# Shared stage rearranged, nine homes for expert weights, square roots in mid-step

## What is computed

```python
# cross-attention: 16 heads of 32, 1601 context rows per sequence
q = qdq(layernorm(x)) @ qdq(wq).T + bq
k, v = split(ctx @ wkv.T + bkv)
x = x + tanh(g_xattn) * (qdq(softmax(q k^T / sqrt(32)) v) @ qdq(wp).T + bp)
# mixture of experts on h = layernorm(x): 32 experts, 4 of them per token
scores = sigmoid(h @ gate_w.T)
top 2 of 4 groups by (scores + gate_bias), then the top 4 experts; weights = scores / sum * 2
slot = running count of tokens per expert, in token order (capacity 128 here)
routed = sum_k weight_k * w2_e(silu(w1_e h) * w3_e h)
shared = (silu(h @ shared_gate) * (h @ shared_up)) @ shared_down
out = x + tanh(g_ffn) * (routed + shared)
```

## Time and profile before

| | us |
|---|---|
| median of 3 runs (lowest, highest) | 3175.16 (3173.58, 3179.16) |
| the profiled execution | 3174.64 |
| its span, first to last instruction | 3172.8 |
| PE busy | 2810.6 (89%) |
| DVE, ACT, POOL busy | 1789.1, 1386.5, 1806.3 |

### The profile page before, as it was taken

One profiled execution on the slowest core, in us unless ns is written; L12 is line 12 of the kernel. 1 busy time (PEld: TensorE's weight loads), 2 busy tenths in 40 slices (PEclk: granted clock), 3 DMA queues, 4 the chain that ended last, 5 costly groups with the idle time before them and its releaser, 6 DMA issues. The chain is left out here.

```text
span 3172.8 us, 43442 instructions
## 1 busy us (share of the span) xinstructions
PE 2810.6 (89%) x14876; PEld 1211.9 (38%) x14876; DVE 1789.1 (56%) x3878; ACT 1386.5 (44%) x2460; POOL 1806.3 (57%) x1570
## 2 busy tenths in 40 slices
PE   5898999899989988998999899989998699996986
PEld 3233333333333333333333333333332354443765
DVE  6576566756665766567567755665653334342221
ACT  3155455644564565455545644564456211010111
POOL 0285567556656676667566656656679032424555
PEclk9798999999999999999999999999999799998999
DMA  3112012210211031112112101211020321222997
GB/s 128 37 45 53 21 35 71 53 31 25 76 53 46 11 101 38 35 40 76 29 34 71 53 21 35 74 53 37 20 65 14 118 71 51 80 80 80 280 290 186
DMA packets 146586, 215.59 MB, mean 68 GB/s; under 512 B 24984, under 2 KB 78232, under 8 KB 146368
## 3 DMA queue, kind: packets, MB, share of 16 engines
q1 hardware_dynamic: 130496, 195.95, 20.5%
q0 software_dynamic: 15872, 16.87, 2.8%
HBM read 126.49 MB, written 34.24 MB: 51 GB/s over the span
## 5 line engine op out<-in xcount | busy, mean ns | idle before, releaser
L1502 POOL TENSOR_TENSOR prob_acc<-prob_acc,probs 128x512 f32<-128x512 f32 x1152 | 1429.3, 1275 | 431.2 <-ACT probs L1031 430.8
L1031 ACT ACTIVATE probs<-s_ps 128x512 f32<-128x512 f32 (+1 forms) x1664 | 937.0, 596 | 758.4 <-PE s_ps L803 727.2
L1245 DVE TENSOR_REDUCE piece_max<-r_all 128x1 f32<-128x400 f32 (+1 forms) x2048 | 1029.2, 566 | 144.9 <-PE r_all L725 138.5
L803 PE MATMUL s_ps<-q_stack,k_flat 97*128 97x512 f16 (+1 forms) x1664 | 633.8, 397 | 66.6 <-ACT probs L1031 58.4
L725 PE MATMUL r_all<-k_flat,q_stack 96*128 96x400 f16 (+1 forms) x2048 | 605.5, 353 | 97.4 <-DVE piece_max L1245 41.2
L817 PE MATMUL o_ps<-probs,v_sb 128*32 128x512 f32 (+1 forms) x3328 | 465.1, 632 | 21.5 <-ACT probs L1031 21.5
L803 PEld LDWEIGHTS s_ps<-q_stack,k_flat 97*128 97x128 f16 (+1 forms) x1664 | 161.3, 101 | 634.8 <-ACT probs L1031 435.7
L1499 POOL COPY prob_acc<-probs 128x512 f32<-128x512 f32 x128 | 72.8, 612 | 490.5 <-PE sum_ps L837 355.9
L725 PEld LDWEIGHTS r_all<-k_flat,q_stack 96*128 96x128 f16 x2048 | 204.4, 101 | 372.5 <-DVE piece_max L1245 122.7
L1534 POOL DMA_INDIRECT slot_rows<-payload,slot x128 | 125.6, 981 | 313.4 <-DVE slot L1432 189.4
L1239 DVE SCALAR_TENSOR_TENSOR k_lo<-r_all,bk_col,k_hi 128x400 f16<-128x400 f32 (+1 forms) x128 | 81.8, 639 | 280.9 <-ACT k_hi L989 280.9
(11 more groups left out here) (193 smaller groups left out, 2719.6 us busy)
## 6 DMA issues: line engine op xcount, KB each, us to landing
k_flat<-k_hi SPq DMA_DIRECT2D x256, 100.1 KB, 2.2
ctx_raw<-in_ctx SPq DMA_DIRECT2D x96, 256.0 KB, 2.8
v_sb<-in_L_ffn_w SPq DMA_DIRECT2D x48, 512.0 KB, 6.3
xin<-in_x SPq DMA_DIRECT2D x16, 1024.0 KB, 5.6
k_flat<-k_lo SPq DMA_DIRECT2D x128, 100.1 KB, 2.2
ctx_hi<-in_L_ffn_w SPq DMA_DIRECT2D x24, 512.0 KB, 6.5
ctx_lo<-in_L_ffn_w SPq DMA_DIRECT2D x24, 512.0 KB, 6.5
q_stack<-q_hi SPq DMA_DIRECT2D x256, 32.0 KB, 1.8
```

The lines of the kernel that those rows point to most:

```text
L803: nc.tensor.matmul(s_ps[j % SBANKS][0:w, :], k_stack[:, g % 2, j, kt * P:kt * P + w], q_stack[:, g % 2, j, :], start=True, stop=True).then ...
L1031: nc.scalar.activation(probs[0:w, slot, j, :], s_ps[j % SBANKS][0:w, :], ACT.Exp).then_inc(probs_ready, 1)
L1245: V.reduce_max(piece_max[:, j * TT + qt, i:i + 1], ps[:, 0:PIECE[i]], X_AXIS).then_inc(free_of(*key), 1)
L1502: last = G.tensor_tensor(prob_acc[:, j, :], prob_acc[:, j, :], probs[:, slot, j, :], ALU.add)
```

## The change

- `ffn_tiles` moves `cum` and `total` behind the second gate and up pair, and puts one `down` tile between the turned h of the next sequence and its logits; the other three `down` tiles come behind the logits.
- On DVE the four routing parts of sequence f + 1 stand between the `add_shared` of sequence f; those of f = 0 come ahead of its first `swiglu`. The slots (`slots_of_experts`) come behind the second `swiglu`.
- `ffn_in` is split. h and x1 of sequences 0 and 1 are loaded ahead of `rows_out(B - 1)`, h of 0 already during the last attention group, into the freed `ctx_lo`; `shared_gate` starts in the last group too.
- Expert weights get 9 homes rather than 4, out of buffers that are free by then; 7 experts are loaded during the shared stage. The slots are read back ahead of the last output. The gathers of the first experts wait for the last `swiglu`, not for the outputs.
- `deviations` goes from the end of its step to behind the second exponential of that step. For the last sequence it goes behind `("logits", 1)`.

```diff
 def ffn_tiles(f):
-    order = gate_tiles(f)
+    gates = gate_tiles(f)
+    order = gates[0:4] + [("cum", f), ("total", f)] + gates[4:]
     if f == 0:
         order += [("oiT", B - 1, c) for c in range(DC)] + [("y", B - 1, t) for t in range(TT)]
-    order += [("cum", f), ("total", f)]
-    order += [("hT", f + 1, c) for c in range(DC)] if f + 1 < B else []
-    order += [("down", f, t) for t in range(TT)]
-    return order + ([("logits", f + 1)] if f + 1 < B else [])
+    down = [("down", f, t) for t in range(TT)]
+    if f + 1 < B:
+        order += [("hT", f + 1, c) for c in range(DC)] + down[0:1] + [("logits", f + 1)]
+        down = down[1:]
+    return order + down
...
-        h_in = (prob_acc[:, :, :], probs[:, 2])
+        h_in = (ctx_lo_flat[:, 0:2 * TT * D].bitcast(FP32).rearrange("p (t d) -> p t d", t=TT), probs[:, 2])
...
+HOMES, EARLY_HOMES, FREE_HOMES = 9, 7, 5
...
             sp.wait_ge(x_quantised, B * TT)
             sp.dma_start(xin[:, :, :], x_v[B - 1]).then_inc(x_again, DMA)
+            key = ("k", B - 1, GROUPS - 1, PIECES - 1)
+            sp.wait_ge(bank_full[ring.last_bank(*key)], ring.done(*key))
+            h_in_of(0)
+            sp.wait_ge(probs_ready, step_of(B - 1, GROUPS - 1, 0) * GH)
+            shared_weights_in(sg, shared_gate)
             sp.wait_ge(acc_summed, B * GROUPS)
-            ffn_in(0)
-            for wt, src in ((sg, shared_gate), (su, shared_up), (sd, shared_down)):
-                sp.dma_start(wt[:, :, :], src.rearrange("(c p) n -> p c n", p=P)).then_inc(shared_in, DMA)
+            shared_weights_in(su, shared_up)
+            h_in_of(1)
+            shared_weights_in(sd, shared_down)
+            for f in range(2):
+                x1_in_of(f)
             rows_out(B - 1)
...
             for f in range(B):
-                if f + 1 < B:
-                    ffn_in(f + 1)
-                if f == B - 2:
-                    expert_weights_in(0)
-                    expert_weights_in(1)
+                if 2 <= f + 1 < B:
+                    h_in_of(f + 1)
+                    x1_in_of(f + 1)
+                if f == 1:
+                    sp.wait_ge(h_out, B * DMA)
+                    sp.wait_ge(x1_out, B * DMA)
+                if 1 <= f <= EARLY_HOMES:
+                    expert_weights_in(f - 1)
+                if f == B - 1:
+                    sp.wait_ge(slots_written, B * TT * TOPK * DMA)
+                    sp.dma_start(e_slots[:, :, :], slot_v).then_inc(e_slots_in, DMA)
                 sp.wait_ge(out_ready, f + 1)
                 sp.dma_start(out_v[f], x1_in[f % 2]).then_inc(out_written, DMA)
             sp.wait_ge(out_written, B * DMA)
             sp.wait_ge(route_ready, B)
-            expert_weights_in(2)
-            expert_weights_in(3)
-            sp.wait_ge(slots_written, B * TT * TOPK * DMA)
-            sp.dma_start(e_slots[:, :, :], slot_v).then_inc(e_slots_in, DMA)
-            for e in range(UN, E):
-                key = ("ey", e - UN)
+            for e in range(EARLY_HOMES, HOMES):
+                expert_weights_in(e)
+            for e in range(HOMES, E):
+                key = ("ey", e - HOMES)
                 sp.wait_ge(bank_full[ring.last_bank(*key)], ring.done(*key))
                 expert_weights_in(e)
...
                 for j in range(GH):
                     exp_of(s, j)
+                    if j == 1 and g == 2 and b + 1 < B and kt == X_STD:
+                        deviations(x_var_ready, b + 2, x_std_ready)
+                    if j == 1 and g == 1 and b and kt == H_STD:
+                        deviations(h_var_ready, b, h_std_ready)
...
-            for f in range(B):
-                for c, part in enumerate((scores_in_groups, best_groups_and_experts, expert_masks, expert_weights)):
-                    swiglu(c)
-                    part()
+            routing = (scores_in_groups, best_groups_and_experts, expert_masks, expert_weights)
+            for part in routing:
+                part(0)
+            for f in range(B):
+                for c in range(FSC):
+                    swiglu(f, c)
+                    if c == FSC // 2 - 1:
+                        slots_of_experts(f)
                 if f == 0:
                     for t in range(TT):
                         tile(("y", B - 1, t))
                     for at in (H_STATS, H_RSTD):
                         h_part(B - 1, at)
+                dve.wait_ge(x1_back[f % 2], (f // 2 + 1) * DMA)
+                for t in range(TT):
+                    if f + 1 < B:
+                        routing[t](f + 1)
+                    add_shared(f, t)
...
             pool.wait_ge(h_out, B * DMA)
-            pool.wait_ge(out_written, B * DMA)
             pool.wait_ge(e_slots_in, DMA)
+            pool.wait_ge(act_ready, B * FSC)
```

More of the change, by code:

```diff
@@ L431, in build @@
         x1_out = sem("x1_out")
-        h_back = sem("h_back")
-        x1_back = sem("x1_back")
+        h_back = [sem(f"h_back{i}") for i in range(2)]
+        x1_back = [sem(f"x1_back{i}") for i in range(2)]
         scores_read = sem("scores_read")
@@ L442, in build @@
         payload_free = sem("payload_free")
-        e_w_in = [sem(f"e_w_in{u}") for u in range(UN)]
+        e_w_in = [sem(f"e_w_in{u}") for u in range(HOMES)]
         e_slots_in = sem("e_slots_in")
@@ L1074, in _ @@
                     tile(key)
-                    if key == ("y", B - 1, TT - 1):
-                        for at in (H_STD,) + H_NORM:
+                    if key == ("logits", 1):
+                        deviations(h_var_ready, B, h_std_ready)
+                        for at in H_NORM:
                             h_part(B - 1, at)
@@ L1432, in _ @@
                 V.tensor_tensor(slot[:, :, :], slotf[:, :, :], over[:, :, :], ALU.add).then_inc(route_ready, 1)
-                for t in range(2, TT):
-                    add_shared(t)
+            routing = (scores_in_groups, best_groups_and_experts, expert_masks, expert_weights)
[6 more added lines that the diff above has]
+                        slots_of_experts(f)
+                if f == 0:
+                    for t in range(TT):
+                        tile(("y", B - 1, t))
+                    for at in (H_STATS, H_RSTD):
+                        h_part(B - 1, at)
+                dve.wait_ge(x1_back[f % 2], (f // 2 + 1) * DMA)
+                for t in range(TT):
+                    if f + 1 < B:
+                        routing[t](f + 1)
+                    add_shared(f, t)
                 for t in range(TT):
@@ L1540, in _ @@
             pool.wait_ge(h_out, B * DMA)
-            pool.wait_ge(out_written, B * DMA)
             pool.wait_ge(e_slots_in, DMA)
+            pool.wait_ge(act_ready, B * FSC)
             def gather(e):
-                key = ("ey", e - UN) if e >= UN else ("down", B - 1, TT - 1)
-                pool.wait_ge(bank_full[ring.last_bank(*key)], ring.done(*key))
+                if e >= UN:
+                    key = ("ey", e - UN)
+                    pool.wait_ge(bank_full[ring.last_bank(*key)], ring.done(*key))
                 step.carry_wait()
@@ L1567, in _ @@
                 gather(e)
+            pool.wait_ge(out_written, B * DMA)
             for e in range(E):
```

78 lines of the change are left out of this document (44 added, 34 removed).

## The result

The changed kernel took 3146.59 us (median of 4 runs, 3140.77 to 3147.65), the kernel before 3176.53 us (4 runs, 3173.58 to 3179.16). The ratio is 0.9904, 95% interval 0.9891 to 0.9917: 30 us faster. The forecast was 3104 us, so 43 us of the expected 71 us of gain are missing, and the time lies above the range of 3080 to 3126. The profiled execution took 3147.53 us, its span 3145.8 us.

A forecast was written before the change was run, and what follows sets the result against it. PE was taken to bound attention and the steady shared stage, DMA engines the experts. Terms of -4, -23, -19, -19 and -6 us sum to -71, taking 3174.6 to 3104 us; 8-in-10 range 3080 to 3126 us.

The forecast's parts named there:

- Roots, -4 us: Attention: roots moved into mid-step gain 0.6 us for each of 7 h roots, 0 for x; -4 us.
- rival 3: Attention: x roots stall PE because ACT waits for late statistics; 16 us lost, 3120 us, chance 0.10.
- Entry and f = 0, -23 us: Entry and first shared sequence: earlier loads and routing start the gates of f = 1 at 2535.5, not 2558.5 us.
- Steady, -19 us: Six steady shared-stage sequences: periods fall from 50.6 to 47.5 us, DVE's work hidden; -19 us, bounds -22 and -8.
- f = 7, -19 us: Last shared sequence to first expert: earlier slots bring gathered rows 49.1 us into it, not 68.1; -19 us.
- Experts, -6 us: Expert stage: more homes let 5 experts go from 7.33 to 6.14 us each; -6 us.
- Rivals 1 and 4: 1: adds follow PE, experts at 6.14 us throughout, 3083 us, chance 0.12; 4: weight loads starve adds, 3194 us, chance 0.02.
- rival 5: f = 7: early reads bring the rows no earlier, PE still idles 25 us; 3123 us, chance 0.04.
- Rival 2: Shared stage: late-freed bank or slow stretches each period keep periods at 50 us; 3119 us, chance 0.12.
- the margin of 2 us: Shared stage: DVE's sigmoid, first routing part and add take 4.9 us; the bank is wanted after 6.9 us.

The follow-up runs named there:

- r13: The kernel before, unchanged, run again for its profile on the chip with late words: 3171.63 us.
- r18: The changed kernel, unchanged, run again on a chip where nothing is late: 3098.82 us, ratio 0.9774.
- e6: The changed kernel with the roots of the steps moved back to the end of their step: 3154.22 us, ratio 0.9928.
- r10: The changed kernel, unchanged, run again on another chip where no copy is late: 3100.97 us, ratio 0.9779.
- r8: The changed kernel, unchanged, run again on the chip with late words: 3145.47 us, ratio 0.9907.
- r9: The kernel before, unchanged, run again for its profile on the chip of r10: 3172.87 us.
- e7: The changed kernel with 4 homes for expert weights, two early experts loaded in sequences 5 and 6: 3146.69 us, ratio 0.9905.
- e1: The changed kernel with POOL's scatters of a sequence held until the next sequence's logits have left PE, payload buffer single: 3126.01 us, ratio 0.9856.
- e3: The changed kernel with the first down tile between the second and third tile of hT: 3158.93 us, ratio 0.9955.
- e5: The changed kernel with scatters held as in e1, plus two buffers each for payload and slots: 3108.24 us, ratio 0.9791.
- e15: The kernel of e5 (changed kernel, held scatters, two buffers) again, beside r14: 3110.87 us, ratio 0.9801.
- r14: The changed kernel, unchanged, run again on the chip of r8: 3148.35 us, ratio 0.9916.
- e16: The kernel before with 14 spare scatters in each of sequences 1 to 6, on the chip with late words: 3185.28 us, ratio 1.0031.
- e11: The changed kernel with all four down tiles behind the logits, on the chip of r10: 3119.75 us, ratio 0.9832.

## Why the prediction was wrong, and where it was right

**The time.** 3104 us was forecast; 3146.6 us was measured. On chips R and S the same kernel takes 3101 and 3099 us against 3170 and 3172 us of before, a ratio of 0.978 as forecast (3104 / 3174.6 = 0.978); on Q it takes 3145 and 3148 us. The profile of the result has the late copies of Q. So the sum held for two chips and failed for the one of the result. There, by profiled spans, the gates of f = 1 start 22.2 us earlier (forecast 27), the steady part is 19.6 us longer (forecast 19 shorter), f = 7 is 18.2 us shorter (forecast 19) and the experts 6.2 us (forecast 6).

**The step that failed** is the steady one: -19 us forecast, +20 us measured. It costed PE, ACT's copies and DVE, and asked only whether DVE keeps up. The slots were moved ahead by half a sequence, and the 16 scatters that POOL issues behind them moved with them, from the last down tiles and the gates to under hT and the logits. The prediction followed them in f = 7 and nowhere else. It took POOL beside PE as free. On Q PE's word that a bank is full comes late under the scatters: in the changed kernel's steady periods 1.0 to 3.0 us late for the copies of hT (up to 7.5 us elsewhere, in r13). And hT, ACT's copy and the logits are the one chain of the period in which PE needs an answer at once. The forecast allowed 0.5 us of slow clock a period, and in the result idle time and slow clock come to 6.9 us a period (53.9 less 47.0). In f = 0 the scatters (2490.9 to 2511.5 us) lie over the way from oiT to y and over the first tile of hT: PE waits 2.91 us for ACT's copy of oiT, where it waits 1.40 us in r18, the first copy of hT starts 3.6 us late, and f = 0 takes 9.5 us longer than in r18. The trace of before could not show the price: in it nothing is late, and on Q, where words are late, its order hides nearly all of it (r13). What could have been read is which short chains the scatters would come to lie over.

**The other terms**, by r18, where nothing is in the way (profiled spans, 3094.4 against 3172.8 us):

- Roots, -4 us: about -6 us (the sums over group 1 under e6), through the mechanism named, 1.79 us on the keys for 2.78 us on the exponential. The same sums show no cost of the x roots, for which rival 3 had 16 us: it is out. By the figures of the Trainium skill (ScalarE: Activation LUTs, What ACT_TABLE_LOAD costs) a root would hold ACT for some 5.6 us, an estimate, and the h roots would gain nothing. The gain of 6 us speaks against that here, and so do the 2.90 us that load, root and load took the earlier trace rows.
- Entry and f = 0, -23 us: -26 us. From PE's last sums of the attention to the first gates it takes 13.3 us rather than 18.8, and f = 0 takes 58.3 us rather than 79.1 (59.5 forecast). At the entry the wait for h is gone, as forecast, and the logits took 4.61 us rather than 7.01: the first 23 of their 32 matmuls came every 0.11 us and the rest every 0.21 us, at half the clock, where in before all came every 0.21 us. The gates of f = 1 start 36.2 us earlier in all (2522.3 for 2558.5). The other 9.9 us are gained in attention, 6 by the roots; the rest lies within what these last sums move from profile to profile (they start at 2453.6 to 2466.5 us in the six profiles with the attention of before, 2449.3 to 2457.0 in the thirteen with the changed one).
- Steady, -19 us: -15 us in r18 (288.7 us) and -12 us in r10 (292.1 us), within the bounds of -22 and -8. A period without slow clock is 47.0 us, as summed. I kept 0.5 us a period for the slow clock behind the logits, and it measured 1.1 and 1.7 us: that is the size that was off. The Trainium skill (TensorE: Matmul & The Clock Gate, HAM oscillation — how this bites in real kernels) has the clock fall in idle gaps; in r18 PE idles for 0.04 us of the steady part and the clock still falls behind some logits, to a mean of 0.98. On Q the gaps come first and the slow stretches are longer (6.8 to 10.2 us, one in each of the result's steady periods; 3.4 or 6.8 us, in three periods of six, in r18), as that rule has it.
- f = 7, -19 us: about -18 us; the rows come 49.9 to 50.8 us into f = 7 of the changed kernel, where 49.1 was forecast.
- Experts, -6 us: 236.1 us in the result, 234.0 in r8, 233.3 in r18, against 242.3 (241 and 239 in r9 and r13), so -9 us in r18 is not clearly more than -6. The pace of adds under the load of weights was right (7.36 for 7.33 us), its end at expert 22 too; behind it nine experts ran at 5.46 us. The price used for the five that gained, 6.14 us, was not the pace without loads: in the trace of before the last four experts ran at (3160.55 - 3141.37) / 4 = 4.80 us (and the add of expert 31 below). That the term still came out is in part luck, since 5 at 6.14 and 4 at 4.80 make 49.9 us and nine at 5.46 make 49.1. Rivals 1 and 4 are out, as is rival 5 by the row of f = 7. The early loads cost nothing that shows (e7).

```profile
3160.55 1.54 POOL L1560 DMA_INDIRECT out_rows<-probs,slot_init  x1 [1.26 <-DMA out_rows<-probs,slot_init]
```

The spans of r18 and before differ by -78.4 us (attention -9.9, entry and f = 0 -26.3, steady -15.2, f = 7 -18.0, experts -9.0), for a forecast of -71. **Rival 2** (50 us a period, chance 0.12) named new waits in the shared stage but in the wrong place: the add behind a routing part never held PE in the changed kernel. It did in e1 and e3, where the order was made tighter. In r18 (sequence 2) that add ends at 2610.7 us, some 2 us before PE starts the down tile that needs the bank: the margin of 2 us was there.

**What stays open.** Why the word of PE comes late on one chip and not on three. That the late words come from the scatters rests on the held kernels: e5 against r8 and e15 against r14, on Q, move the scatters (and give them buffers), and the late copies of hT and 37 us go; the late words then come where the scatters now lie. It is not the loads of weights (e7), nor the roots (e6), nor the order by itself (r10 and r18 have it, and nothing is late). How the scatters delay a word is not known, nor why only tiles that end some way into a row of them have late words. Whether it is their number, their rows or their completions was not tried, nor whether another core of the chip would show it, nor what else the machine did at the time: Q was measured in two groups 25 minutes apart, the others in one each.

## What to carry to other kernels

When a step is moved, list what its followers on every engine will lie over, the DMA issues of POOL among them, and look there for chains in which PE needs an answer within a microsecond or two (transpose, copy, multiply). Keep indirect scatters off such chains even if the trace at hand shows no price: here, holding them behind the logits cost nothing on one chip and was worth 37 us on another. A hold needs its own buffers (e1 against e5), and a kernel whose time rests on short answers is worth a profile on more than one chip.

## What the hardware showed that was not expected

- The same kernel took 3099 and 3101 us on two chips and 3145 to 3148 us on a third (1.5%), where the kernel before took 3170 to 3176 us on all four: 0.2% apart.
- On the third chip the semaphore of a finished PE tile reached ACT late while POOL's indirect scatters ran: by 1 to 3 us for hT in the steady periods of the changed kernel, by 5.3 to 7.5 us for the logits in the kernel before (r13), and not at all for tiles that ended in the first 7 us of a row of scatters (e16). PE's own logits matmuls stood still by up to 2.4 us between two of one tile. With the scatters held, hT and the logits went through without a pause (e5).
- The place of one down tile was worth 19 us on a chip with nothing late (e11 against r10): 1 us of waiting a period, and slow clock behind it.
